# Attention round: narrow and wide maxima in one pair, value products in pieces of 128 columns

## The reference

```python
x = x + tanh(g_xattn) * attention(layernorm(x), ctx, ctx)     # 32 query heads, 8 key/value groups, head size 16, causal
x = x + tanh(g_ffn) * moe(layernorm(x))                       # 16 experts, top 4 in 2 of 4 groups, plus a shared expert

# attention, per batch b and group g, the 4 heads h of the group share k and v
scores = einsum('bnghd,bmgd->bnghm', q, k) / 4                # 512 x 512 for each head, causal
attn = softmax(scores); out = einsum('bnghm,bmgd->bnghd', attn, v)
```

## Time and profile before

| what | us |
|---|---|
| median of 3 runs | 1684.65 |
| lowest and highest run | 1676.1 and 1688.54 |
| the profiled execution, its own time | 1688.83 |
| its span, first to last instruction | 1686.8 |
| attention in it, first maximum to last copy | 225 to 589.4 |
| mean granted TensorE clock | 0.87 |

### The profile page before, as it was taken

How to read it: one execution, slowest core, us unless ns; L and a number is a source line. 1 busy time by engine, 2 the same in 40 slices (tenths; PEclk the granted TensorE clock), 3 DMA queues, 4 the chain that set the end, 5 groups by cost and what they waited for, 6 DMA issues and landing times. The chain is left out here.

```text
span 1686.8 us, 28607 instructions
## 1 busy us (share of the span) xinstructions
PE 1348.6 (80%) x8380; PEld 965.6 (57%) x8381; DVE 755.0 (45%) x1939; ACT 533.9 (32%) x951; POOL 613.2 (36%) x810
## 2 busy tenths in 40 slices
PE   6566089889989836735399999999989995999996
PEld 3233064333333313435399998988888884675673
DVE  2112047888787314458503533443353520344343
ACT  1101015555555500110155554544444442100100
POOL 4111002333332200000267776775666774042232
PEclk9877589999898767855699999998999997998897
DMA  5434222333232154620344444443533533052342
GB/s 184 129 118 137 86 72 68 91 97 98 71 99 77 42 171 153 221 102 0 133 128 126 132 132 159 137 126 109 175 113 113 194 103 137 13 175 66 109 148 75
DMA packets 100017, 194.97 MB, mean 116 GB/s; under 512 B 27044, under 2 KB 28580, under 8 KB 98952
## 3 DMA queue, kind: packets, MB, share of 16 engines
q1 hardware_dynamic: 71400, 118.35, 21.9%
q0 software_dynamic: 17200, 55.38, 11.2%
q10 hardware_dynamic: 11376, 20.71, 3.2%
HBM read 130.07 MB, written 64.03 MB: 115 GB/s over the span
## 5 line engine op out<-in xcount | busy, mean ns | idle before, releaser
L421 DVE CUSTOM_DVE_ANT_0 a_mb<-a_mb,late 128x384 f32<-128x384 f32 (+3 forms) x512 | 244.1, 513 | 109.6 <-PE a_mb L458 102.2
L1044 DVE CAST e_w<-e_w 128x480 fp32r<-128x480 f32 x144 | 99.2, 699 | 319.2 <-DMA e_w<-in_w2T 319.1
L400 ACT ACTIVATE a_at<-a_eb 128x1024 f32<-128x1024 f32 (+3 forms) x256 | 178.5, 705 | 179.1 <-PE a_eb L476 179.1
L344 POOL TENSOR_SCALAR_AFFINE_SELECT a_at<-a_at 128x256 f32<-128x256 f32 x256 | 104.5, 408 | 331.1 <-ACT a_at L400 331.1
L1181 PE MATMUL e_gate<-e_w,e_xT 128*128 x948 | 178.0, 339 | 39.0 <-DVE e_w L1052 34.6
L1181 PEld LDWEIGHTS e_gate<-e_w,e_xT 128*128 128x128 f32 x948 | 165.2, 200 | 50.6 <-issue 39.8
L1200 PE MATMUL e_yps<-e_w,e_hT 128*128 x711 | 185.5, 404 | 1.9 <-ACT e_hT L1113 1.4
L1181 PE MATMUL e_up<-e_w,e_xT 128*128 x948 | 174.7, 334 | 0.0
L1181 PEld LDWEIGHTS e_up<-e_w,e_xT 128*128 128x128 f32 x948 | 154.2, 193 | 0.0
L490 PE MATMUL a_pv<-a_at,a_v 128*32 128x256 f32 (+3 forms) x2048 | 133.1, 335 | 14.5 <-POOL a_at L344 8.6
L1200 PEld LDWEIGHTS e_yps<-e_w,e_hT 128*128 128x128 f32 x711 | 128.1, 189 | 27.3 <-issue 1.6
(11 more groups left out here) (194 smaller groups left out, 1785.7 us busy)
## 6 DMA issues: line engine op xcount, KB each, us to landing
e_w<-in_w13T SPq DMA_DIRECT2D x16, 1408.0 KB
dy<-e_y ACTq DMA_DIRECT2D x79, 256.0 KB
dq<-p_parts SPq DMA_DIRECT2D x48, 256.0 KB
a_q<-dq SPq DMA_DIRECT2D x64, 192.0 KB
do<-a_o SPq DMA_DIRECT2D x32, 256.0 KB, 3.5
dx<-c_x POOLq DMA_DIRECT2D x8, 1024.0 KB, 8.2
e_w<-in_w2T SPq DMA_DIRECT2D x16, 512.0 KB
a_k<-dk SPq DMA_DIRECT2D x64, 98.0 KB
```

Of the source, the lines that this page charges most:

```text
L344: eng.affine_select(out=square, in_=square, compare_op=ALU.is_ge, fill=0.0, base=0, pattern=[[0, 2], [1, P]], channel_multiplier=-1).then_ ...
L400: eng.activation(at[r % 2][:, ch, 2 * hp:2 * hp + 2, ch * P:SEQ], eb[hp][:, :, ch * P:SEQ], ACT.Exp, scale=0.25).then_inc(s_exp, 1)
L421: eng.tensor_tensor_reduce(out=b[:, 0:w], in0=b[:, 0:w], in1=io["late"][:, SEQ - w:SEQ], scale=1.0, scalar=3 * NEG, op0=ALU.add, op1=ALU.m ...
L1044: eng.tensor_copy(w[rows, r, 0, cols], w[rows, r, 1, cols].bitcast(F32)).then_inc(s_high, 1)
```

## The change

PAIRS gives for each turn two entries (t, ch): every pair now joins a narrow chunk and a wide one, 0 with 3 or 1 with 2, the narrow one first. Turns 0 and 1 have the narrow one at t = 0, turns 2 and 3 at t = 1. The sum of the widths of a round is as before. exp_unit computes only columns from min(ch * 128, 256) on: 512, 384, 256 and 256 columns. VALUES gives for each unit (slot) the pieces of products (late, chunk, first and last block of 128 columns); late = 1 is the round before. Units 0 to 7 now have 128, 128 + 128, 256, 128, 128, 128, 128 and 128 columns; chunk 1 comes in units 5, 6 and 7, chunk 2 in units 0 and 1 of the next round, chunk 3 in unit 1. The spins behind the pairs before round 0 are 10 each, the same sum.

```diff
--- before.py
+++ after.py
@@ -270,7 +270,10 @@
 def stage_attend(nc, io, dram):
 
     AHEAD, SPIN, FILL, RING = 2, 96, 24, 3
-    ORDER, SKIPPED, TURNED = (0, 3, 2, 1), HG, HG + 1
+    SKIPPED, TURNED = HG, HG + 1
+    PAIRS = (((0, 0), (1, 3)), ((0, 1), (1, 2)), ((1, 0), (0, 3)), ((1, 1), (0, 2)))
+    VALUES = (((1, 2, 2, 3),), ((1, 2, 3, 4), (1, 3, 3, 4)), ((0, 0, 0, 2),), ((0, 0, 2, 3),), ((0, 0, 3, 4),),
+              ((0, 1, 1, 2),), ((0, 1, 2, 3),), ((0, 1, 3, 4),))
     with ExitStack() as c:
         sb = lambda n, s, d=F32: c.enter_context(nc.sbuf_tensor(n, s, d))
         ps = lambda n, s: c.enter_context(nc.psum_tensor(n, s, F32))
@@ -317,8 +320,8 @@
         def exists(i):
             return not isinstance(i, int) or i < NIT
 
-        def place(turn, j, t):
-            n = turn * HG + 2 * j + t
+        def place(turn, j, at):
+            n = turn * HG + 2 * j + at
             return n if n < SKIPPED else n + 2
 
         def bank(p):
@@ -408,13 +411,11 @@
             eng.reg_mov(due, (NB + AHEAD) * CH * HG + 2)
 
             def maxima(i, r, turn):
-                ch = ORDER[turn]
-                w = (ch + 1) * P
                 for j in range(2):
-                    for t in range(2):
-                        h, b = head(t, j), bank(place(turn, j, t))
+                    for at, (t, ch) in enumerate(PAIRS[turn]):
+                        h, b, w = head(t, j), bank(place(turn, j, at)), (ch + 1) * P
                         if isinstance(i, int):
-                            eng.wait_ge(s_smax, i * CH * HG + turn * HG + 2 * j + t + 2)
+                            eng.wait_ge(s_smax, i * CH * HG + turn * HG + 2 * j + at + 2)
                         else:
                             eng.wait_ge(s_smax, eng.snap(due))
                             eng.reg_add(due, due, 1)
@@ -446,16 +447,14 @@
         def _(eng):
             def max_pair(i, r, turn, j):
 
-                ch = ORDER[turn]
-                w = max(256, (ch + 1) * P)
                 u = i * CH * HG + turn * HG + 2 * j
                 if place(turn, j, 1) - RING == SKIPPED:
                     eng.wait_ge(s_rmax, u + 1)
                 elif not isinstance(i, int) or u:
                     eng.wait_ge(s_rmax, u)
-                for t in range(2):
-                    rows = slice(HALF * t, HALF * t + ROW_MAX)
-                    eng.matmul(bank(place(turn, j, t))[:, 0:w], q[r][rows, j, ch * P:(ch + 1) * P], k[r][rows, 0:w], start=True, stop=True).then_inc(s_smax, 1)
+                for at, (t, ch) in enumerate(PAIRS[turn]):
+                    rows, w = slice(HALF * t, HALF * t + ROW_MAX), max(256, (ch + 1) * P)
+                    eng.matmul(bank(place(turn, j, at))[:, 0:w], q[r][rows, j, ch * P:(ch + 1) * P], k[r][rows, 0:w], start=True, stop=True).then_inc(s_smax, 1)
 
             def turn_maxima(i, r, done):
                 eng.wait_ge(s_rmax, done)
@@ -468,29 +467,32 @@
 
             def exp_unit(i, r, ch, j):
 
+                n0 = min(ch * P, 256)
                 eng.wait_ge(s_exp, i * 2 * CH + 2 * ch + j)
                 if not after(i, 1):
                     spin(eb[j][:, 0], FILL)
                 for t in range(2):
                     rows = slice(HALF * t, HALF * t + ROW_MAX + 1)
-                    mm = eng.matmul(eb[j][:, t], k[r][rows, ch * P:(ch + 1) * P], q[r][rows, j, :], start=True, stop=True)
+                    mm = eng.matmul(eb[j][:, t, n0:SEQ], k[r][rows, ch * P:(ch + 1) * P], q[r][rows, j, n0:SEQ], start=True, stop=True)
                 mm.then_inc(s_sexp, 1)
 
-            def pv_unit(i, r, ch, part):
-
-                w = (SEQ - ch * P) // 2
-                cols = slice(ch * P + part * w, ch * P + (part + 1) * w)
-                if part == 0:
-                    eng.wait_ge(s_causal, i * 2 * CH + 2 * ch + 3)
-                    if ch == 0:
-                        eng.wait_ge(s_o, i + 1)
-                for j in range(2):
-                    for t in range(2):
-                        h = head(t, j)
-                        mm = eng.matmul(pv[32 * h:32 * h + 32, cols], v[r][:, ch, :], at[r % 2][:, ch, 2 * j + t, cols],
-                                        start=ch == 0 and part == 0, stop=ch == CH - 1, skip_group_check=True, tile_position=(0, 32 * h))
-                if ch == CH - 1 and part == 1:
-                    mm.then_inc(s_pv, 1)
+            def pv_units(i, r, slot):
+
+                for late, ch, n0, n1 in VALUES[slot]:
+                    if not after(i, late):
+                        continue
+                    of, buf, cols = i - late, (r - late) % 2, slice(n0 * P, n1 * P)
+                    if n0 == ch:
+                        eng.wait_ge(s_causal, of * 2 * CH + 2 * ch + 3)
+                        if ch == 0:
+                            eng.wait_ge(s_o, of + 1)
+                    for j in range(2):
+                        for t in range(2):
+                            h = head(t, j)
+                            mm = eng.matmul(pv[32 * h:32 * h + 32, cols], v[(r - late) % NB][:, ch, :], at[buf][:, ch, 2 * j + t, cols],
+                                            start=ch == 0 and n0 == 0, stop=ch == n1 - 1, skip_group_check=True, tile_position=(0, 32 * h))
+                    if ch == CH - 1:
+                        mm.then_inc(s_pv, 1)
 
             spin(pv, SPIN)
             for i in range(AHEAD):
@@ -498,7 +500,7 @@
                 for turn in range(CH):
                     for j in range(2):
                         max_pair(i, i, turn, j)
-                        spin(pv, 4 * (ORDER[turn] + 1))
+                        spin(pv, 10)
                     if turn == 0 and i:
                         turn_maxima(0, 0, CH * HG + HG)
 
@@ -511,15 +513,12 @@
                         if exists(i + AHEAD):
                             max_pair(i + AHEAD, (r + AHEAD) % NB, ch, j)
                         exp_unit(i, r, ch, j)
-                        if ch:
-                            pv_unit(i, r, ch - 1, j)
-                        elif after(i, 1):
-                            pv_unit(i - 1, (r - 1) % NB, CH - 1, j)
+                        pv_units(i, r, 2 * ch + j)
                     if ch == 0 and exists(i + 1):
                         turn_maxima(i + 1, r + 1, (i + AHEAD) * CH * HG + HG if exists(i + AHEAD) else NIT * CH * HG + 1)
             steps(eng, body)
-            for part in range(2):
-                pv_unit(NIT - 1, NB - 1, CH - 1, part)
+            for slot in range(2):
+                pv_units(NIT, NB, slot)
 
 
 def stage_close(nc, io, dram):
```

## The result

| | before | changed |
|---|---|---|
| median, us | 1686.6 (4 runs) | 1779.44 (4 runs) |
| lowest, highest | 1676.1, 1700.51 | 1779.1, 1780.43 |
| ratio, 95% interval | | 1.0546, 1.0468 to 1.0624 |
| the profiled execution, its span | 1688.83, 1686.8 | 1779.71, 1777.7 |
| attention: first pair to last copy | 225 to 589.4 | 223.2 to 672.9 |

The span grew by 90.9 us. Up to the last copy of the attention 83.5 came in. Behind it, where nothing was changed, it was 7.4; the mean clock there is 0.87 in both profiles, and the cause of the 7.4 was not looked for.

A forecast was written before the change was run, and what follows sets the result against it. The prediction took the attention to be bound by TensorE's pairs and VectorE's maxima waiting for each other. From 1688.83 us it took 28.3 for shorter rounds and 9.9 for vanished clock falls: 1650.6, taken as 1649, range 1638 to 1666.

The forecast's parts named there:

- The hand-over: Attention, TensorE's pairs and VectorE's maxima waiting for each other: 0.96 us a unit in turns 0 and 2, 1.09 in 1 and 3.
- the prices: Attention steps at 2.4 GHz: pair to exp_unit 0.22 to 0.34 us, 256 product columns 0.57, maxima 0.28 and 0.68.
- the walk: One loop round added up unit by unit, each start set by the latest wait: 9.15 us instead of 10.08.
- still released by the copy: Sign to look for: unit 2's products wait for ScalarE's copy, due 3.39 us into the round.
- the second rival: Attention pairs: narrow and wide members run one after the other, rounds 9.43 us, total 1659 or 1669; chance 0.13.
- The 0.06 a unit set aside for weight loads in turn 2: By the Trainium skill's rule, exposed weight loads cost turn 2 0.06 us twice a round, 3.5 in all, giving 1652.5.
- end early enough: Loads in the attention's rounds finish in time for a round of 9.15 us, so they set no new bound.
- the trough: TensorE's lightest part of a round: streaming rises from 42% to 47%, called denser and taken to keep the clock up.
- the falls to go away: Two drops to 1.2 GHz in the attention's loop vanish, saving 9.9 us.
- The slower rival: Attention rounds stay at 1.2 GHz for long, 13.5 us each; 1714 with half of 29 rounds low; chance 0.04.
- the break-even at 8.8 low rounds: Attention rounds at 1.2 GHz cost 4.35 us more each, so the 38.2 won is gone from 8.8 on.
- The falls that stay: Rival: the clock still falls in the attention, so only 28.3 us are saved, total 1660; chance 0.25.

The follow-up runs named there:

- e9: Changed kernel, load of v on its own semaphore, useless matmuls at the start of rounds 2 and 3 and behind round 3: 1637.71 to 1777.51 us, six runs.
- e13: Changed kernel with round 3 serialised, every unit waiting for GpSimd's square of the unit before: 1770.02 to 1784.42 us, four runs.
- e14: Changed kernel with each pair's narrow member as wide as the wide one, and round 3 serialised: 1698.25 to 1781.76 us, four runs.
- e15: Changed kernel with equal pair widths, all 512 score columns and round 3 serialised: 1686.83 to 1722.86 us, ten runs, median 1691.59.
- e3: Kernel before with the narrow-and-wide pairs alone: 1751.36 to 1797.0 us, four runs.
- e2: Kernel before with the shorter score columns alone: 1732.35 to 1746.83 us, four runs, ratio 1.0323.
- e4: Kernel before with the spread products alone: 1706.48 to 1728.61 us, four runs, ratio 1.0192.
- e12: Kernel before with round 3 serialised, every unit waiting for GpSimd's square of the unit before: 1694.09 to 1731.09 us, four runs.
- e6: Changed kernel with all 512 score columns and the load of v on its own semaphore: 1645.93 to 1808.02 us, six runs.
- e1: Changed kernel with all 512 score columns in every exp_unit again: 1652.67 to 1811.37 us, four runs.
- e8: Changed kernel with each pair's narrow member computed as wide as the wide one: 1653.43 to 1753.85 us, four runs.
- e7: Changed kernel with 3, 4 and 4 useless matmuls ahead of the exp_units of units 3, 6 and 7: 1667.26 to 1683.12 us, ten runs, ratio 0.992.
- e10: e9 with each pair's narrow member as wide as the wide one: 1661.58 to 1698.95 us, six runs, ratio without the last 0.9859.
- e11: e10 with all 512 score columns: 1659.78 to 1668.44 us, four runs, ratio 0.9849.

## Why the prediction was wrong

- **The hand-over, the prices and the walk** hold at 2.4 GHz: 9.28 against 9.15 (e9, with its own semaphore for v). Units 3 to 7 and 0 and 1 are within 0.02 each, the unit 1 that ends with a 512 maximum included (1.65 against 1.64). From a pair to its scores are 0.22 whatever the width, and the wider member's columns show behind the scores instead; the sums of both hold. Only unit 2 is off: its products start 0.83 after the pair, not 0.71, and it takes 1.40 instead of 1.28. The sign "still released by the copy" was misread from the start: the earlier trace rows and e9 both name GpSimd's square. In e9 it ends at 401.23 and the copy at 401.16, so both are near the limit. Unequal widths do run beside each other: the second rival is out. The 0.06 a unit set aside for weight loads in turn 2 did not show either: 0.96 was measured both times.
- **Loads "end early enough"** failed. I had it from a round of the loop; in round 1 TensorE was released by the load of v 5.2 us after its issue, having waited 1.51.
- **The step that failed is the clock.** The prediction filled the trough (0.51 us of streaming in 1.09 instead of 0.46 in 0.96 to 1.24) and took the falls to go away, 9.9 us won and no low round left. The profile shows 28 low rounds of 13.54 instead of 9.15, 123 us more than the sum had. Two things were wrong in it. It counted columns at the time they take TensorE, so a pair with half of its rows idle counted full. And it looked at the high rounds only. Once low, a round is TensorE-bound and its matmuls show no idle time. Whether the clock comes back then goes with what the array does in the round (e13, e14, e15), and there the change takes away on all three sides: beside the wide member half of the rows stand idle (alone, e3: no return), 1280 score columns for each half are dropped (alone, e2: no return), and the products are levelled (alone, e4: a return after five rounds instead of one).
- **The slower rival was right in what happens and in its price, in part in its reason, and wrong in its chance.** Its reason was the shorter scores, which are one of the three. It gave 13.5 us for a low round; 13.54 was measured. It gave the break-even at 8.8 low rounds, and rounds 2 to 29 were low. With 28 the same working gives 1650.6 + 28 x 4.35 = 1772.4; the profiled execution took 1779.71. Its chance stood at 0.04 because of the "denser trough". The trace of before had shown twice that this stage's clock can fall without any gap, and that should have been worth far more.
- The falls that stay (0.25) were priced at 5.0 us each, by the return that the kernel before makes after some 17 us. That price was the old rounds' price, and does not carry over.

The low clock for nearly the whole stage is shown (the stretches). So is the lost return (e12 against e13), and that array work beside the wide member and the score columns together bring it back (e15). What lets the clock fall stays open. It fell behind waits of 1.2 to 1.7 us (the changed kernel, e6, e13, e14), did not behind waits as long (1.19 in e1, 1.37 in e8), and fell without any in the kernel before, in e2 and in e4. What made e9 fall in four of six runs with both places covered is not known, since its profiled run did not fall. Open is also how much of the missing falls in e7, e10 and e11 comes from their longer rounds of 9.7 to 10.06 rather than from the added work.

## A version that beats both

e10 and e11 are 1.4 and 1.5% faster than the kernel before (e10 without its slowest run), little, but with both intervals below 1, and all their runs but one of e10 lie below the lowest of the 11 runs of before beside them (1675.53). e11 computes more than it needs in both places and is none the worse: both have rounds of 9.7. e9 shows what is left on the table, 1637.71 in its best run, if the clock could be held.

## What to carry to other kernels

- Columns without use can be worth their time on TensorE. Before work is cut from TensorE, look whether it is on the path; if a hand-over sets the pace, the cut gains nothing and may cost the clock for the stage.
- Look in the profile at each fall of the clock, also short ones: how the stage comes back is a property of its rounds at the *lower* level. Price a fall with the rounds of the changed kernel, and force one by serialising a single round.
- Time several runs and list them. One kernel here gave 1652.67 and 1811.37; a single run would have shown either.

## What the hardware showed that was not expected

- Two stable levels of one program, 9.36 and about 14.6 us a round (copies of e1 and e6, the same rounds but for a semaphore), with no way back over 400 us in e6's profile, although TensorE was busy throughout.
- A matmul in the idle half of the rows, beside one that runs anyway, costs no time and helps the clock, though not surely: back after some 3 us in e8, in some of four runs of e14, never in the changed kernel or e13.
- Four 128-column fillers between half-row matmuls cost 0.49 us (e7), twice their own 0.22.
- The clock can fall in full work and stay down: e2 fell at 320, with no wait of TensorE above 0.40 us in the round before, and stayed low for the rest of the stage.
